# Second attention of a two-block transformer kernel: one query copy, each head's matmuls on its own 32 partitions

## Chip, cores and metric

The kernel runs on one core of a Trainium2 chip. The metric is the device time of one execution in microseconds (us). Before the change it is 2706.89 us, the median of 3 runs (2706.29 to 2707.69).

## What is computed

The input is a sequence of 2048 tokens of 128 features. Two pre-normed blocks follow each other: `x = x + attn1(layernorm(x))`, then `x = x + block2(layernorm(x))`.

The first attention has 16 heads of 64 features, with sinusoidal positions added to the keys. The second block is an attention with 16 heads of 8 features, an output projection, a layernorm, a router that gives each token one of four experts (relu MLPs with 512 hidden features) and a second layernorm. What matters here is its attention:

```python
q = (src @ Wq + bq).reshape(B, T, N_HEAD, HEAD_DIM)   # 2048 tokens, 16 heads of 8
k = (src @ Wk + bk).reshape(B, T, N_HEAD, HEAD_DIM)
v = (src @ Wv + bv).reshape(B, T, N_HEAD, HEAD_DIM)
scale = HEAD_DIM ** (-0.5)
scores = jnp.einsum('bqhd,bkhd->bhqk', q, k) * scale
probs = jax.nn.softmax(scores, axis=-1)
attn = jnp.einsum('bhqk,bkhd->bqhd', probs, v).reshape(B, T, D_MODEL)
```

All is float32. In the second block the query side's features are 8 per head; the kernel splits each float into a high part and a rest to keep precision in single-pass (fp32r) matmuls, so that a head takes 24 rows plus one row for the maximum, of 32.

## The kernel before

The kernel is written by hand engine by engine; its order is the order of the code, and semaphores tie the engines together. It has a startup and a loop for the first attention (to about 1590 us), a startup (1592 to 1674 us) and a loop (1674 to 2540 us) for the second, and a tail with the experts.

**Layout of the second attention.** The 16 heads make four groups of four. A group's keys lie in `k4` (line 167), 128 partitions by 2048 tokens: head h of the group has partitions 32h to 32h+31, of which 8 hold the high part, 8 the rest, 8 the high part again, and row 24 (`MROW`) a one. Queries come in 4 chunks of 512 tokens. They lie in `q4` (line 168), which takes up all of `kb`: for every chunk four copies of 128 partitions by 512, one per head, where only that head's 32 partitions are filled and the others are zero. So a matmul with all 128 rows of `k4` and one head's copy gives that head's scores. GpSimd zeroes `q4` once (line 758). VectorE computes a chunk's queries into `stage_q` by three operations (`parts2` and line 1120), and SP copies the four heads' 32 rows each by DMA (`move_q2`, lines 855 to 859). The row 24 of each copy gets minus the maximum of each query's scores (`move_m2`, line 861), so the exponential needs no further subtraction.

**Maxima.** Before a chunk's scores can be used, the maximum of each query's scores over all keys must be known. For the next chunk 64 tiles are computed (`max_tile2`, line 351): 4 heads x 4 query tiles of 128 x 4 key chunks of 512. Each is one matmul of 512 columns into a bank of `ring` (three PSUM banks, `RING = 3`), which VectorE reduces over its columns (line 993) and so releases. A tile may be written only when the tile three uses ahead of it has been released: `side()` (line 302) waits on `side_free` for that, for every use of the ring: tiles, query, key and value projections (lines 328, 342), the transposes of the output (line 527) and the finish of the maxima (line 360). TensorE and VectorE walk through the same list, `side_items2` (line 99), in the order of `TILES2` (line 96): all of head 0's tiles, then head 1's, and so on.

**The loop.** 16 chunks (4 groups x 4 query chunks), 16 steps each, one step per 128 keys. In step t TensorE runs the code of lines 565 to 587:

- `scores2` of step t+1 for heads 0 and 1 (two matmuls with 128 keys as weights and 512 queries as columns, line 511), once ScalarE has read these banks' former content;
- a part of the step's side items; `scores2` for heads 2 and 3; two more parts;
- `values2` of step t (line 518): four heads x two passes, 128 keys by 16 value columns, accumulated in `acc_o`, once ScalarE's exponentials of step t (line 676, two per step, 1024 columns each) are done;
- the last part of the side items.

The side items, 4 tiles in a plain step, are shared out evenly: `parts = share(on_pe(items), 4)`, so one of four tiles stands between the scores, one behind them and one ahead of the values, and one behind the values. Step 1 has the output transposes in addition, step 3 a query projection ("Q"), steps 6 and 10 key projections ("K") in the first two chunks of a group, step 6 the value projection ("V") in the third, step 12 the reduction over the key chunks ("mred") and the finish ("fin"), which transposes the maxima. From step 12 on the tiles are those of the chunk after the next ("early").

The startup computes the first chunk's queries, all the keys and values of the first group, then the first chunk's 64 tiles and 16 early ones.

Of the kernel before, what the change touches and what calls it, by code (L numbers as in the profile page):

```python
# [18 lines left out]
F32 = mybir.dt.float32  # L19
# [9 lines left out]
CW = 512  # L29
NC = S // CW  # L30
# [62 lines left out]

MAX2_STEPS = 12
EARLY2 = 4 * (STEPS2 - MAX2_STEPS)
TILES2 = [(h, q, k) for h in range(4) for q in range(QT) for k in range(NC)]


def side_items2(c, first):
# [49 lines left out]
def build(nc, x, w_pairs, wout_pairs, bqk_pairs, bv_pairs, b_out, pos, w_groups, bqk_groups, bv_groups,  # L149
          coefs, w_o, b_o, router_w, router_b, w1, b1, w2, b2, ln1_g, ln1_b, ln2_g, ln2_b, identity, out):  # L150
    ctx = ExitStack()
    with ctx:
# [12 lines left out]


        k4 = ka[:, :, 0, :]
        q4 = kb[:].rearrange("p a h n -> p (a h n)").rearrange("p (c h n) -> p c h n", c=NC, h=4)
        v1 = sb("v1", [128, 2, NT, 128])
        v1_flat = v1[:].rearrange("p a t n -> p (a t n)")  # L170
        v2_flat = v1_flat[:, 0:2 * NT * 4 * VW]
# [75 lines left out]
        exp2_done = [sem(f"exp2_done{h}") for h in range(2)]  # L247
        pv2_done, o2_copied, rs2_ready = sem("pv2_done"), sem("o2_copied"), sem("rs2_ready")
        mx2_ready, m2_dma = sem("mx2_ready"), sem("m2_dma")
        q2_part, q2_ready, q2_dma = sem("q2_part"), sem("q2_ready"), sem("q2_dma")  # L250
        k2_part, k2_ready = sem("k2_part"), sem("k2_ready")

        ld3, w2_ld, hid_ready = sem("ld3"), sem("w2_ld"), sem("hid_ready")
# [45 lines left out]
        def _(pe):  # L299
# [50 lines left out]

            def max_tile2(par, c, h, q, k):
                bank = side()
                nc.tensor.matmul(bank[:], q4[:, c, h, q * 128:(q + 1) * 128], k4[:, par, k * CW:(k + 1) * CW],  # L353
                                 start=True, stop=True).then_inc(side_full, 1)

            def fin(ready, count, n):
# [132 lines left out]
            for it in on_pe(start_items2()):  # L489
                kind = it[0]  # L490
                if kind == "Q":
                    proj(0, 0, it[1] * CW)
                elif kind == "K":
                    proj(0, 1, it[1] * CW)
                elif kind == "V":
                    proj_v2(0)
                elif kind == "max":
                    if it[1:] == TILES2[0]:
                        pe.wait_ge(q2_dma, 64)
                        pe.wait_ge(k2_ready, NC)  # L500
                    max_tile2(0, 0, *it[1:])
                elif kind == "early":
                    pe.wait_ge(q2_dma, 128)
                    max_tile2(0, 1, *it[1:])
                else:
                    fin(mx2_ready, 1, 16)

            def scores2(G, par, c, u, t):
                pe.wait_ge(exp2_done[u], 1 + STEPS2 * G + t)
                for k in range(2):  # L510
                    last = nc.tensor.matmul(sc[u][:, k, :], k4[:, par, t * 128:(t + 1) * 128], q4[:, c, 2 * u + k, :],  # L511
                                            start=True, stop=True)
                last.then_inc(sc2_ready[u], 1)

# [34 lines left out]

            def early_ready(g, c, G):  # L550

                pe.wait_ge(q2_dma, 64 * (G + 3))
                if c == 2:
                    pe.wait_ge(k2_ready, NC * (g + 2))

# [3 lines left out]
            with pe.Fori(0, GROUPS // 2) as i:  # L559
                rebase(LOOP2 + BODY2 * i, LOOP2 % RING)  # L560
                for k in range(2 * NC):
                    par, c = k // NC, k % NC
                    g = 2 * i + par
                    G = NC * g + c
                    for t, items in enumerate(side_items2(c, k == 0)):
                        parts = share(on_pe(items), 4)
                        nxt = (G, par, c, t + 1) if t < STEPS2 - 1 else (G + 1, (k + 1) // NC % 2, (k + 1) % NC, 0)
                        if t == STEPS2 - 1:
                            pe.wait_ge(m2_dma, 64 * (G + 2))
                        scores2(nxt[0], nxt[1], nxt[2], 0, nxt[3])  # L570
                        if t == MAX2_STEPS:
                            early_ready(g, c, G)
                        for it in parts[0]:
                            item2(it, g, par, c, k, G)
                        scores2(nxt[0], nxt[1], nxt[2], 1, nxt[3])
                        for it in parts[1]:
                            item2(it, g, par, c, k, G)
                        if t == 0:
                            pe.wait_ge(o2_copied, 1 + G)
                        for it in parts[2]:  # L580
                            item2(it, g, par, c, k, G)
                        for u in range(2):
                            pe.wait_ge(exp2_done[u], 1 + STEPS2 * G + t + 1)
                        values2(par, t, 0)
                        values2(par, t, 1).then_inc(pv2_done, 1)
                        for it in parts[3]:
                            item2(it, g, par, c, k, G)
                o_rows(G, k)


# [120 lines left out]
        def _(pool):  # L711
# [43 lines left out]
            pool.wait_ge(m_dma, 32 * (NC * PAIRS + 1))  # L755
            pool.wait_ge(q_dma, 96 * (NC * PAIRS + 2))
            pool.wait_ge(k_dma, 96 * NC * (PAIRS + 1))
            nc.gpsimd.memset(kb[:].rearrange("p a h n -> p (a h n)").bitcast(F32), 0.0).then_inc(init2, 1)
            nc.gpsimd.memset(v2_flat, 0.0).then_inc(init2, 1)
            pool.wait_ge(init2, 2)  # L760
            nc.gpsimd.memset(v2_flat.rearrange("p (x n) -> p x n", n=VW)[:, :, D2:D2 + 1], 1.0).then_inc(init2, 1)


# [1 line left out]
        def _(sp):  # L765
# [86 lines left out]
                sp.dma_start(tail_rows[:, 6 + e, :], b2[e:e + 1, :].to_broadcast([128, DM])).then_inc(ld3, 16)  # L852
            sp.dma_start(rb_sb[:], router_b[None, :].to_broadcast([128, 1])).then_inc(ld3, 16)

            def move_q2(n, c):
                sp.wait_ge(q2_ready, n + 1)
                for h in range(4):
                    rows = slice(32 * h, 32 * h + 32)
                    sp.dma_start(q4[rows, c, h, :].bitcast(F32), stage_q[rows, 0, :].bitcast(F32)).then_inc(q2_dma, 16)

            def move_m2(c, served):
                sp.wait_ge(side_free, served)
                for h in range(4):
                    sp.dma_start(q4[32 * h + MROW:32 * h + MROW + 1, c, h, :].bitcast(F32), m_rows[QT * h:QT * (h + 1), :].bitcast(F32)).then_inc(m2_dma, 16)

            sp.wait_ge(init2, 3)
            move_q2(0, 0)
            move_q2(1, 1)
            move_m2(0, START2 + NC + on_pe(start_items2()).index(("fin",)) + 1)
            with sp.Fori(0, GROUPS // 2) as i:  # L870
                for k in range(2 * NC):
                    par, c = k // NC, k % NC
                    g = 2 * i + par
                    G = NC * g + c
                    move_q2(G + 2, (c + 2) % NC)
                    if c == 2:
                        load_group(g + 2, par)
                    move_m2((c + 1) % NC, served2(i, k, "fin"))
# [1 line left out]
            sp.wait_ge(side_free, START3)  # L880

            sp.wait_ge(m2_dma, 64 * (NC * GROUPS + 1))
            sp.wait_ge(q2_dma, 64 * (NC * GROUPS + 2))
            sp.wait_ge(w2_dma, 48 * (GROUPS + 2))
            for e in range(E):
                sp.dma_start(w2_sb[:, e], w2[e].rearrange("(f k) n -> k f n", k=128)).then_inc(w2_ld, 16)
# [9 lines left out]
        def _(dve):  # L896
# [213 lines left out]
                dve.wait_ge(part, part_count)  # L1110
                done_so_far()

            def q2_proj(n, par):
                if not (isinstance(n, int) and n == 0):
                    dve.wait_ge(q2_ready, n)
                bank = side()
                parts2(bank, bqk_sb[:, par, 0:1], 0, stage_q[:, 1, :], accs[:, 0, :], q2_part, n + 1)
                if not (isinstance(n, int) and n == 0):
                    dve.wait_ge(q2_dma, 64 * n)
                nc.vector.scalar_tensor_tensor(stage_q[:, 0, :], stage_q[:, 1, :].bitcast(F32), coef_sb[:, 1:2],  # L1120
                                               accs[:, 0, :], ALU.mult, ALU.add).then_inc(q2_ready, 1)

            def k2_proj(n, par, c):
# [13 lines left out]
            for it in start_items2():  # L1137
                kind = it[0]
                if kind == "Q":
                    q2_proj(it[1], 0)  # L1140
                elif kind == "K":
                    k2_proj(it[1], 0, it[1])
                elif kind == "V":
                    dve.wait_ge(init2, 3)
                    v2_proj(0)
                elif kind == "mred":
                    mred(4, mx2_ready, mxp2[0])
                elif kind == "fin":
                    fin(0, 4, m2_dma)
                else:  # L1150
                    max_tile(*it[1:], mxp2[kind == "early"])
# [12 lines left out]
            with dve.Fori(0, GROUPS // 2) as i:  # L1164
                rebase(LOOP2 + BODY2 * i, LOOP2 % RING)
                for k in range(2 * NC):
# [3 lines left out]
                    for items in side_items2(c, k == 0):  # L1170
                        for it in items:
# [7 lines left out]
                            elif kind == "fin":  # L1179
                                fin(G + 1, 4, m2_dma)  # L1180
                            elif kind == "Q":
                                q2_proj(G + 2, par if c < 2 else 1 - par)
                            elif kind == "K":
                                if it[1] == 0:
                                    dve.wait_ge(w2_dma, 48 * (g + 2))
                                k2_proj(NC * (g + 1) + it[1], 1 - par, it[1])
                            elif kind == "V":
                                v2_proj(1 - par)
                            else:
                                o_rows(G - 1, g if c else g - 1, (c - 1) % NC)  # L1190
# [153 lines left out]
```

## Time and profile before

| | |
|---|---|
| median of 3 runs | 2706.89 us |
| span of the profiled execution | 2706.8 us |
| TensorE busy (PE) | 2573.3 us, 95% |
| weight loads (PEld) | 1447.8 us, 53% |
| VectorE busy (DVE) | 2049.9 us, 76% |
| ScalarE busy (ACT) | 1106.3 us, 41% |
| GpSimd busy (POOL) | 851.5 us, 31%, none of it after 1602 us |
| mean granted TensorE clock | 0.966 |
| DMA, mean share of the 16 engines | 11.1% |

The profile is of one execution, 2706.8 us from the first to the last instruction, 0.1 us from the median. Busy time of an engine is the time in which at least one of its instructions runs; matmuls are pipelined, so TensorE can be busy throughout and still have room, and the duration of one matmul (about 0.4 us for 512 columns) is longer than the distance to the next. L353 means line 353 of the kernel. The idle time of a group is that of its engine just ahead of it, with the engine and line that ended it. The granted clock is in parts of 2.4 GHz; 0.50 is 1.2 GHz.

### The profile page before, as it was taken

The numbers are of one execution on the slowest core, as the hardware profiler recorded it, in microseconds if no ns is written. First come the engines' busy times: TensorE is split into PE (matmuls) and PEld (weight loads), VectorE is DVE, ScalarE is ACT, GpSimd is POOL, SyncE is SP. The second block draws the span as 40 slices with busy tenths as digits, with TensorE's granted clock in tenths as the row PEclk, the third lists the DMA queues.
The fourth block names the chain that finished last, engine by engine and source line by source line (L and its number), as shares of the span: only waits on it lengthen the run. The fifth ranks groups of instructions, "written<-read, shape, count | busy, mean of one in ns | idle before, by whom it ended". The sixth has DMA issues, their size and how long they took to land. (4 is left out here: it accounts for less than half of the span.)

```text
span 2706.8 us, 39054 instructions
## 1 busy us (share of the span) xinstructions
PE 2573.3 (95%) x11918; PEld 1447.8 (53%) x11918; DVE 2049.9 (76%) x3471; ACT 1106.3 (41%) x1150; POOL 851.5 (31%) x405
## 2 busy tenths in 40 slices
PE   4999999999999999999999969999999999999796
PEld 2555555555555565555555544455455445455465
DVE  6767777676767767677776779988888888898834
ACT  0333333333333333343333311556556555665332
POOL 3463645646554645636465520000000000000000
PEclk8999999999999999999999976999999999999898
DMA  4120211211211201102112110000000000000000
GB/s 113 36 52 12 48 41 25 47 29 28 55 29 34 54 13 42 46 13 48 41 24 54 34 36 5 9 7 5 7 10 5 6 5 11 5 5 8 20 0 16
DMA packets 54408, 73.00 MB, mean 27 GB/s; under 512 B 12968, under 2 KB 23872, under 8 KB 54080
## 3 DMA queue, kind: packets, MB, share of 16 engines
q1 hardware_dynamic: 54208, 70.46, 11.1%
q8 instruction: 109, 1.79, 0.3%
q14 instruction: 91, 0.75, 0.1%
HBM read 9.33 MB, written 1.05 MB: 4 GB/s over the span
## 5 line engine op out<-in xcount | busy, mean ns | idle before, releaser
L993 DVE TENSOR_REDUCE mxp<-ring 128x1 f32<-128x512 f32 x1640 | 1068.3, 685 | 341.3 <-PE ring L348 292.4
L655 ACT ACTIVATE prob<-scores 128x1024 f32<-128x1024 f32 x512 | 524.0, 1025 | 902.1 <-PE scores L393 877.4
L676 ACT ACTIVATE prob<-scores 128x1024 f32<-128x1024 f32 x512 | 496.8, 1022 | 414.5 <-PE scores L511 414.3
L740 POOL TENSOR_TENSOR accp<-accp,prob 128x1024 f32<-128x1024 f32 x256 | 598.1, 2370 | 0.0
L400 PE MATMUL acc_o<-prob,v 128*64 128x512 f32 x2048 | 506.3, 616 | 0.0
L353 PE MATMUL ring<-ka,kb 128*128 128x512 f32 x1104 | 448.7, 450 | 9.9 <-DVE accs L1109 3.6
L392 PE MATMUL scores<-qa,ka 128*128 128x512 f32 x1028 | 425.7, 414 | 4.6 <-issue 3.1
L348 PE MATMUL ring<-ka,qa 128*128 128x512 f32 x1064 | 417.1, 436 | 11.9 <-DMA kb<-stage_k 7.9
L393 PE MATMUL scores<-qb,kb 65*128 65x512 f32 x1028 | 407.4, 396 | 0.0
L993 DVE TENSOR_REDUCE accs<-ring 128x1 f32<-128x512 f32 x528 | 343.5, 686 | 50.6 <-PE ring L353 49.7
L353 PEld LDWEIGHTS ring<-ka,kb 128*128 128x128 f32 x1104 | 213.7, 195 | 312.9 <-DVE mxp L993 132.7
L511 PE MATMUL scores<-kb,ka 128*128 128x512 f32 x1028 | 338.6, 411 | 4.5 <-ACT prob L676 4.5
L348 PEld LDWEIGHTS ring<-ka,qa 128*128 128x128 f32 x1064 | 192.2, 193 | 252.4 <-issue 106.5
L737 POOL TENSOR_TENSOR accp<-prob 128x1024 f32<-128x1024 f32 x64 | 151.3, 2364 | 549.9 <-DVE accs L1071 549.9
L518 PE MATMUL acc_o<-prob,v 128*16 128x512 f32 x2048 | 271.1, 601 | 0.0
L400 PEld LDWEIGHTS acc_o<-prob,v 128*64 128x64 f32 x2048 | 125.7, 137 | 237.8 <-issue 201.3
L392 PEld LDWEIGHTS scores<-qa,ka 128*128 128x128 f32 x1028 | 195.7, 190 | 57.2 <-issue 15.9
L511 PEld LDWEIGHTS scores<-kb,ka 128*128 128x128 f32 x1028 | 193.1, 190 | 53.1 <-issue 15.4
L393 PEld LDWEIGHTS scores<-qb,kb 65*128 65x128 f32 x1028 | 194.9, 190 | 48.0 <-issue 7.7
L1031 DVE TENSOR_TENSOR accp<-accp,prob 128x1024 f32<-128x1024 f32 x130 | 161.7, 1245 | 0.0
L1081 DVE SCALAR_TENSOR_TENSOR x<-ring,rs,x 128x128 f32<-128x128 f32 x264 | 74.3, 344 | 75.3 <-PE ring L421 75.3
L328 PE MATMUL ring<-xnt,w_sb 128*128 128x512 f32 x216 | 118.3, 635 | 4.6 <-issue 0.9
(105 smaller groups left out, 1366.1 us busy)
## 6 DMA issues: line engine op xcount, KB each, us to landing
ka<-stage_k SPq DMA_DIRECT2D x144, 128.0 KB, 2.3
qa<-stage_q SPq DMA_DIRECT2D x136, 128.0 KB, 2.3
kb<-stage_k SPq DMA_DIRECT2D x72, 128.0 KB, 2.3
qb<-stage_q SPq DMA_DIRECT2D x68, 128.0 KB, 2.3
kb<-stage_q SPq DMA_DIRECT2D x72, 64.0 KB, 2.0
w_sb<-w_pairs SPq DMA_DIRECT2D x10, 192.0 KB, 2.4
kb<-m_rows SPq DMA_DIRECT2D x68, 2.0 KB
qb<-m_rows SPq DMA_DIRECT2D x66, 2.0 KB
```

The costliest lines, as they stand in the source:

```text
L348: nc.tensor.matmul(bank[:], qa[:, c, h, q * 128:(q + 1) * 128], ka[:, par, h, k * CW:(k + 1) * CW], start=True, stop=True).then_inc(side_f ...
L353: nc.tensor.matmul(bank[:], q4[:, c, h, q * 128:(q + 1) * 128], k4[:, par, k * CW:(k + 1) * CW], start=True, stop=True).then_inc(side_full, 1)
L392: nc.tensor.matmul(sc[h][:, k, :], ka[:, par, h, keys_of], qa[:, c, h, :], start=True, stop=False)
L393: last = nc.tensor.matmul(sc[h][:, k, :], kb[0:D1 + 1, par, h, keys_of], qb[0:D1 + 1, c, h, :], start=False, stop=True)
L400: last = nc.tensor.matmul(acc_o[64 * h:64 * h + 64, :], v1[:, par, t, 64 * h:64 * h + 64], prob[:, h, j % 4, k, :], start=(t == 0), stop=( ...
L511: last = nc.tensor.matmul(sc[u][:, k, :], k4[:, par, t * 128:(t + 1) * 128], q4[:, c, 2 * u + k, :], start=True, stop=True)
L518: last = nc.tensor.matmul(acc_o[32 * h:32 * h + VW, :], v2[:, par, t, h, :], prob[:, u, t % 4, k, :], start=(t == 0), stop=(t == NT - 1))
L655: nc.scalar.activation(prob[:, h, j % 4, :, :], sc[h][:, :, :], ACT.Exp, scale=SCALE1).then_inc(exp_done[h], 1)
L676: nc.scalar.activation(prob[:, u, t % 4, :, :], sc[u][:, :, :], ACT.Exp, scale=SCALE2).then_inc(exp2_done[u], 1)
L740: nc.gpsimd.tensor_tensor(accp[:, h], accp[:, h], prob[:, h, j % 4], ALU.add).then_inc(pool_acc[h], 1)
L993: nc.vector.reduce_max(partial[:, h * QT + q, k:k + 1], bank[:], AX.X).then_inc(side_free, 1)
L1031: nc.vector.tensor_tensor(accp[:, h], accp[:, h], prob[:, h, j % 4], ALU.add).then_inc(done[h], 1)
```

## The change

The queries are kept once, not four times. Head h's score and maximum matmuls read only partitions 32h to 32h+31 of both operands (a contraction over 32 rows, not 128). The tiles' order becomes: for each query tile and key chunk, heads 2, 3, 0, 1. The side items of a step are shared into two parts, not four: after the scores of heads 0 and 1 come the first half (in a plain step the tiles of heads 2 and 3), after those of heads 2 and 3 the second (heads 0 and 1), and then the values. VectorE writes a chunk's queries straight to `q2`. The 72 copying DMAs, their semaphore `q2_dma` and the zeroing of `kb` go; the DMA of the maximum rows, one per head, stays.

```diff
-TILES2 = [(h, q, k) for h in range(4) for q in range(QT) for k in range(NC)]
+TILES2 = [(h, q, k) for q in range(QT) for k in range(NC) for h in (2, 3, 0, 1)]
...
-        q4 = kb[:].rearrange("p a h n -> p (a h n)").rearrange("p (c h n) -> p c h n", c=NC, h=4)
+        q2 = kb[:, 0, 0, :].rearrange("p (c n) -> p c n", c=NC)
...
             def max_tile2(par, c, h, q, k):
                 bank = side()
-                nc.tensor.matmul(bank[:], q4[:, c, h, q * 128:(q + 1) * 128], k4[:, par, k * CW:(k + 1) * CW],
+                rows = slice(32 * h, 32 * h + 32)
+                nc.tensor.matmul(bank[:], q2[rows, c, q * 128:(q + 1) * 128], k4[rows, par, k * CW:(k + 1) * CW],
                                  start=True, stop=True).then_inc(side_full, 1)
...
                 pe.wait_ge(exp2_done[u], 1 + STEPS2 * G + t)
                 for k in range(2):
-                    last = nc.tensor.matmul(sc[u][:, k, :], k4[:, par, t * 128:(t + 1) * 128], q4[:, c, 2 * u + k, :],
+                    rows = slice(32 * (2 * u + k), 32 * (2 * u + k) + 32)
+                    last = nc.tensor.matmul(sc[u][:, k, :], k4[rows, par, t * 128:(t + 1) * 128], q2[rows, c, :],
                                             start=True, stop=True)
                 last.then_inc(sc2_ready[u], 1)
...
-                        parts = share(on_pe(items), 4)
+                        parts = share(on_pe(items), 2)
...
                         if t == 0:
                             pe.wait_ge(o2_copied, 1 + G)
-                        for it in parts[2]:
-                            item2(it, g, par, c, k, G)
                         for u in range(2):
                             pe.wait_ge(exp2_done[u], 1 + STEPS2 * G + t + 1)
                         values2(par, t, 0)
                         values2(par, t, 1).then_inc(pv2_done, 1)
-                        for it in parts[3]:
-                            item2(it, g, par, c, k, G)
...
-            nc.gpsimd.memset(kb[:].rearrange("p a h n -> p (a h n)").bitcast(F32), 0.0).then_inc(init2, 1)
             nc.gpsimd.memset(v2_flat, 0.0).then_inc(init2, 1)
...
-            def move_q2(n, c):
-                sp.wait_ge(q2_ready, n + 1)
-                for h in range(4):
-                    rows = slice(32 * h, 32 * h + 32)
-                    sp.dma_start(q4[rows, c, h, :].bitcast(F32), stage_q[rows, 0, :].bitcast(F32)).then_inc(q2_dma, 16)
-
             def move_m2(c, served):
                 sp.wait_ge(side_free, served)
                 for h in range(4):
-                    sp.dma_start(q4[32 * h + MROW:32 * h + MROW + 1, c, h, :].bitcast(F32), m_rows[QT * h:QT * (h + 1), :].bitcast(F32)).then_inc(m2_dma, 16)
+                    sp.dma_start(q2[32 * h + MROW:32 * h + MROW + 1, c, :].bitcast(F32), m_rows[QT * h:QT * (h + 1), :].bitcast(F32)).then_inc(m2_dma, 16)
...
-                nc.vector.scalar_tensor_tensor(stage_q[:, 0, :], stage_q[:, 1, :].bitcast(F32), coef_sb[:, 1:2],
+                nc.vector.scalar_tensor_tensor(q2[:, c, :], stage_q[:, 1, :].bitcast(F32), coef_sb[:, 1:2],
                                                accs[:, 0, :], ALU.mult, ALU.add).then_inc(q2_ready, 1)
```

What waited for `q2_dma` (the first tiles of a chunk on TensorE, the next query chunk on VectorE, SP at the end) now waits for `q2_ready` or for nothing.

## Rows read from the trace of the kernel before

**Rows 1.** The windows view: busy us of PE, PEld, DVE, ACT, POOL; clock, DMA, GB/s.
```profile
1630.00:1660.00 30.00, 30.00 (x52) 14.46 (x51) 30.00 (x51) 0.00 (x0) 0.00 (x0) 0.50 0.02 5
1674.00:2540.00 866.00, 850.83 (x4375) 436.19 (x4375) 752.27 (x1192) 508.98 (x530) 0.00 (x0) 0.99 0.03 7
```

**Rows 2.** The groups by line, in the second attention's loop (1676 to 2540 us).
```profile
L353 PE MATMUL ring<-ka,kb 128*128 128x512 f32 x1024 | 401.9, 426 | 7.1 <-DVE accs L1109 3.0 <-DVE stage_kf L1109 3.0
L511 PE MATMUL scores<-kb,ka 128*128 128x512 f32 x1024 | 337.5, 411 | 4.5 <-ACT prob L676 4.5
L993 DVE TENSOR_REDUCE accs<-ring 128x1 f32<-128x512 f32 x513 | 334.4, 686 | 50.5 <-PE ring L353 49.5 <-issue 0.3
L993 DVE TENSOR_REDUCE mxp<-ring 128x1 f32<-128x512 f32 x512 | 333.6, 686 | 37.7 <-PE ring L353 37.4
L518 PE MATMUL acc_o<-prob,v 128*16 128x512 f32 x2048 | 271.1, 601 | 0.0
```

**Rows 3.** The waits in the same loop: us in total, times, longest.
```profile
ACT prob L676 <- PE scores L511: 414.3, 257, 72.2
```

**Rows 4.** The timeline of a plain step: start us, us, engine, line, operation [idle before].
```profile
1785.80 0.13 PEld L518 LDWEIGHTS acc_o<-prob,v 128*16 128x16 f32 x8 [0.35 <-ACT prob L676]
...
1786.78 0.50 PE L353 MATMUL ring<-ka,kb 128*128 128x512 f32 x1
...
1787.32 2.67 DVE L993 TENSOR_REDUCE accs<-ring 128x1 f32<-128x512 f32 x4 [0.35 <-PE ring L353]
...
1788.05 0.42 PEld L353 LDWEIGHTS ring<-ka,kb 128*128 128x128 f32 x2
1788.28 0.61 PE L353 MATMUL ring<-ka,kb 128*128 128x512 f32 x2
1788.82 0.13 PEld L518 LDWEIGHTS acc_o<-prob,v 128*16 128x16 f32 x8 [0.35 <-ACT prob L676]
```

**Rows 5.** The timeline of VectorE in the second attention's startup.
```profile
1627.47 38.35 DVE L993 TENSOR_REDUCE mxp<-ring 128x1 f32<-128x512 f32 x64
```

**Rows 6.** The DMA view's issues (KB, us to landing); GpSimd's timeline ahead of the startup.
```profile
kb<-stage_q SPq DMA_DIRECT2D x72, 64.0 KB, 2.0
...
1592.94 6.93 POOL L758 MEMSET kb<- 128x8192 f32 x1 [25.60 <-DVE x L1081]
```

**Rows 7.** Windows of line 421, first attention's end: PE (x), PEld (x), clock, DMA, GB/s.
```profile
1588.36:1589.38 1.02, 0.96 (x4) 0.96 (x5) 0.50 0.00 0
1589.38:1590.83 1.45, 1.45 (x12) 1.45 (x11) 0.50 0.00 0
```

**Rows 8.** The timeline of two steps around a query projection.
```profile
2122.53 0.13 PEld L518 LDWEIGHTS acc_o<-prob,v 128*16 128x16 f32 x8 [0.35 <-ACT prob L676]
...
2124.91 0.75 DVE L1108 TENSOR_SCALAR stage_q<-ring,bqk_sb 128x512 fp32r<-128x512 f32 x1 [0.17 <-PE ring L328]
...
2125.58 0.80 DVE L1109 TENSOR_SCALAR accs<-ring,bqk_sb,coef_sb 128x512 f32<-128x512 f32 x1
...
2126.43 0.19 PEld L353 LDWEIGHTS ring<-ka,kb 128*128 128x128 f32 x1 [0.61 <-DVE accs L1109]
...
2126.86 0.13 PEld L518 LDWEIGHTS acc_o<-prob,v 128*16 128x16 f32 x8 [0.25 <-issue]
...
2127.24 4.27 DVE L993 TENSOR_REDUCE accs<-ring 128x1 f32<-128x512 f32 x7
...
2130.21 0.13 PEld L518 LDWEIGHTS acc_o<-prob,v 128*16 128x16 f32 x8 [0.25 <-ACT prob L676]
```

**Rows 9.** The timeline of weight loads: values behind a step with transposes; around a finish.
```profile
1792.29 0.13 PEld L518 LDWEIGHTS acc_o<-prob,v 128*16 128x16 f32 x8 [0.36 <-ACT prob L676]
...
2090.85 0.13 PEld L518 LDWEIGHTS acc_o<-prob,v 128*16 128x16 f32 x8 [0.35 <-ACT prob L676]
...
2097.05 0.13 PEld L518 LDWEIGHTS acc_o<-prob,v 128*16 128x16 f32 x8 [0.24 <-ACT prob L676]
```

**Rows 10.** Line 353 in the startup at the lower clock (min/median/max ns).
```profile
L353 PE MATMUL ring<-ka,kb x18: 792/794/796, 1639.6 to 1649.7; 128*128 128x512 f32 x18
```

More of the change, by code:

```diff
@@ L249, in build @@
         mx2_ready, m2_dma = sem("mx2_ready"), sem("m2_dma")
-        q2_part, q2_ready, q2_dma = sem("q2_part"), sem("q2_ready"), sem("q2_dma")
+        q2_part, q2_ready = sem("q2_part"), sem("q2_ready")
         k2_part, k2_ready = sem("k2_part"), sem("k2_ready")
@@ L498, in _ @@
                     if it[1:] == TILES2[0]:
-                        pe.wait_ge(q2_dma, 64)
+                        pe.wait_ge(q2_ready, 1)
                         pe.wait_ge(k2_ready, NC)
@@ L502, in _ @@
                 elif kind == "early":
-                    pe.wait_ge(q2_dma, 128)
+                    pe.wait_ge(q2_ready, 2)
                     max_tile2(0, 1, *it[1:])
@@ L550, in early_ready @@
             def early_ready(g, c, G):
-                pe.wait_ge(q2_dma, 64 * (G + 3))
+                pe.wait_ge(q2_ready, G + 3)
                 if c == 2:
@@ L757, in _ @@
             pool.wait_ge(k_dma, 96 * NC * (PAIRS + 1))
-            nc.gpsimd.memset(kb[:].rearrange("p a h n -> p (a h n)").bitcast(F32), 0.0).then_inc(init2, 1)
             nc.gpsimd.memset(v2_flat, 0.0).then_inc(init2, 1)
-            pool.wait_ge(init2, 2)
+            pool.wait_ge(init2, 1)
             nc.gpsimd.memset(v2_flat.rearrange("p (x n) -> p x n", n=VW)[:, :, D2:D2 + 1], 1.0).then_inc(init2, 1)
@@ L863, in move_m2 @@
                 for h in range(4):
-                    sp.dma_start(q4[32 * h + MROW:32 * h + MROW + 1, c, h, :].bitcast(F32), m_rows[QT * h:QT * (h + 1), :].bitcast(F32)).then_inc(m2_dma, 16)
-            sp.wait_ge(init2, 3)
-            move_q2(0, 0)
-            move_q2(1, 1)
+                    sp.dma_start(q2[32 * h + MROW:32 * h + MROW + 1, c, :].bitcast(F32), m_rows[QT * h:QT * (h + 1), :].bitcast(F32)).then_inc(m2_dma, 16)
             move_m2(0, START2 + NC + on_pe(start_items2()).index(("fin",)) + 1)
@@ L874, in _ @@
                     G = NC * g + c
-                    move_q2(G + 2, (c + 2) % NC)
                     if c == 2:
@@ L882, in _ @@
             sp.wait_ge(m2_dma, 64 * (NC * GROUPS + 1))
-            sp.wait_ge(q2_dma, 64 * (NC * GROUPS + 2))
             sp.wait_ge(w2_dma, 48 * (GROUPS + 2))
@@ L1111, in parts2, with q2_proj @@
                 done_so_far()
-            def q2_proj(n, par):
+            def q2_proj(n, par, c):
                 if not (isinstance(n, int) and n == 0):
@@ L1117, in q2_proj @@
                 parts2(bank, bqk_sb[:, par, 0:1], 0, stage_q[:, 1, :], accs[:, 0, :], q2_part, n + 1)
-                if not (isinstance(n, int) and n == 0):
-                    dve.wait_ge(q2_dma, 64 * n)
-                nc.vector.scalar_tensor_tensor(stage_q[:, 0, :], stage_q[:, 1, :].bitcast(F32), coef_sb[:, 1:2],
+                nc.vector.scalar_tensor_tensor(q2[:, c, :], stage_q[:, 1, :].bitcast(F32), coef_sb[:, 1:2],
                                                accs[:, 0, :], ALU.mult, ALU.add).then_inc(q2_ready, 1)
@@ L1139, in _ @@
                 if kind == "Q":
-                    q2_proj(it[1], 0)
+                    q2_proj(it[1], 0, it[1])
                 elif kind == "K":
@@ L1143, in _ @@
                 elif kind == "V":
-                    dve.wait_ge(init2, 3)
+                    dve.wait_ge(init2, 2)
                     v2_proj(0)
@@ L1181, in _ @@
                             elif kind == "Q":
-                                q2_proj(G + 2, par if c < 2 else 1 - par)
+                                q2_proj(G + 2, par if c < 2 else 1 - par, (c + 2) % NC)
                             elif kind == "K":
```

## The prediction

> **What bounds the kernel now.** I read the busy time by stretch first. Only the second attention is touched, so its loop has to be explained: 866 us of the 2706.8 us span, TensorE busy 850.8, VectorE 752.3, ScalarE 509.0, at a granted clock of 0.99 [rows 1]. In the groups by line TensorE's time there is 1024 maximum tiles (402 us), 1024 score matmuls (338 us) and 2048 value matmuls (271 us) [rows 2]. The waits agree: exponentials wait for scores, 414 us (72 of it once, ahead of the loop) [rows 3], and reductions for a tile, 49.5 + 37.4 us [rows 2]. ScalarE, busy 59% of the loop, can't be the bound.
>
> A plain step in the timeline shows how it runs. From one values block to the next is 3.02 us (1785.80 to 1788.82). The eight 512-column matmuls ahead of the values follow each other 0.23 us apart (the last two tiles: weight load 1788.05, matmul 1788.28). From the values to the next weight load it takes 0.98 us (1785.80 to 1786.78). VectorE's four reductions take 2.67 us of it, and it idles 0.35 us ahead of the first [rows 4]. TensorE is the bound, VectorE close behind: back to back it does 64 reductions in 38.35 us, 0.60 us each, 2.40 us a step [rows 5].
>
> **The change, part by part.**
>
> *Copies, DMAs, memset gone.* 72 DMAs from SP (2.0 us to landing each) and one memset of 6.93 us [rows 6]. A chunk's copies are made after step 3 and first read in step 12. The memset ends at 1599.87 [rows 6]; the value tile that waits for it stands just ahead of the 64 startup tiles, which begin at 1627.47 [rows 5]. I cost all of it at 0: without that cover it would be 7 us, once. VectorE's three operations for a query chunk stay, with another destination; the maximum row's four DMAs stay; nothing is moved past another on a queue.
>
> *Row groups.* Head h now reads partitions 32h to 32h+31 alone. Does the array run such matmuls side by side? For column groups the value matmuls show it: 601 ns each, yet 2048 in 271 us, 132 ns apiece [rows 2]. For row groups there is one place: the end of the first attention, where the output matmuls of the two 64-row halves come one behind the other. While the first half's run alone, four take 1.02 us; with the second half's beside them, twelve take 1.45 us, 0.12 us apiece at the same clock of 0.50, with eleven weight loads [rows 7]. Matmuls and weight loads of different row groups overlap. So four in a row (score, score, tile, tile, on four different groups) are one pass of 0.23 us here, loads side by side. The other end is no overlap at all, 0.23 us each. Between them: matmuls overlap, loads go one by one, at 0.11 us if four in 1.02 us at half clock [rows 7] are the pace of loads. I take the first end, the nearest row.
>
> The Trainium skill (TensorE: Matmul & The Clock Gate, Part 3) has measured 3.07 times, not 4, for four 32-row matmuls of 512 columns. By it a pass takes some 0.07 us more and the sum below loses about 18 us. No run here has groups of 32 rows.
>
> *The order of a step* decides how much of that arrives. Before, one of the four tiles went behind the values; now all four go ahead: S0 S0 m1 m2, S1 S1 m3 m4, values. The ring has three banks, so m4 waits until VectorE has released m1 of the same step, and the values are queued behind m4. The chain, from a step's first weight load:
> - m1's load 0.05 (estimate: two loads close together ahead of it), its matmul 0.50, hand-over to VectorE 0.04 (1786.78 + 0.50 to 1787.32) [rows 4]: its reduction starts at 0.59.
> - The reduction 0.69 [rows 2], release to the waiting load 0.05 (VectorE's operation ends at 2126.38, the tile that waited for it loads at 2126.43) [rows 8]: m4 loads at 1.33.
> - From a load that had to wait to the values 0.43 (2126.43 to 2126.86) [rows 8], values to the next load 0.98 [rows 4].
>
> Sum 2.74 us, 0.28 less than 3.02, though TensorE's own work falls by more than 1 us. ScalarE's two exponentials (509 us over 256 steps, 2.0) [rows 1] and VectorE's 2.40 fit in.
>
> *Steps with more in them.* A query or key projection waits for m2's release (0.59 + 0.60 + 0.69 + 0.05 = 1.93); VectorE starts on it at about 3.1 and takes 2.33 (2124.91 to 2127.24) [rows 8]. The next m1 is reduced only at 5.4, its m4 loads at 6.1, and the step after begins 1.41 later, at 7.5. Before, such a pair took 7.68 (2122.53 to 2130.21) [rows 8]: gain 0.15. A step with output transposes: o waits for the same 1.93, four transposes 0.6, values 0.98: 3.5, before 3.47 (1788.82 to 1792.29) [rows 4, 9]: 0. The finish of the maxima: before 6.20 for two steps (2090.85 to 2097.05) [rows 9]; after, fin stands behind the reduction of all maxima and e4 behind e2, which I put at 6.1 to 6.3: 0. The value projection is one long TensorE piece before and after: 0.
>
> *Sum.* 256 steps: 32 projection pairs (64), 15 with transposes, 16 with a finish (8 of them with a plain neighbour), 4 value projections, about 1 at the loop's turn: 148 plain. 148 x 0.28 = 41.4, 32 x 0.15 = 4.8: 46 us. Startup tiles run at VectorE's 0.60 us either way [rows 5]. 2706.8 - 46 = 2661. The span lies 0.1 us from the median of the runs (2706.89), so nothing is corrected.
>
> **Rivals.**
>
> *Loads one by one.* m1's load comes at 0.22 and the chain is 2.93: 148 x 0.09 = 13 won, some 0.05 to 0.25 lost in each special step, 11 in all: about 2704, no change. Against it: the eleven loads in 1.45 us [rows 7]. Chance 0.07.
>
> *No overlap (slower).* m1 stands behind two scores, so its reduction starts at 1.0, not 0.59, m4 loads at 1.74, the step takes 3.15. The tile that used to hide behind the values is then pure loss: 148 x 0.13 = 19, pairs 7.95 (9), transposes (7), finishes and value projections (10): 2752. It decides from where m1's reduction starts later than about 0.80 after the first load. For it: what rows 7 show is groups of 64 rows, not of 32. That the matmuls don't land on separate groups at all is the same case. Chance 0.09.
>
> *The clock falls (slower).* With one tile per 0.6 us in the startup the granted clock stood at 0.50, the 1.2 GHz level; in the dense loop it is at 0.99, near all of it at 2.4 GHz [rows 1]. The new step leaves TensorE without a matmul for about 0.6 us while m4 waits, and each matmul uses a quarter of the rows. At half clock a tile takes 0.79 [rows 10] and the values block would double, the step comes to about 4.3, 1.55 more: 30 of 256 steps there eat the whole gain. With a quarter of them, 2661 + 99 = 2760. Against it: the startup had 512 columns in 0.6 us, the new loop has well over twice that. The Trainium skill (TensorE: Matmul & The Clock Gate, Part 1) says that activity releases the throttle and that it is back when the engine idles: this rival; the trace agrees with its two levels. Chance 0.10.
>
> *m4's wait is hidden.* Were the chain shorter than VectorE's work, a plain step would be 2.40: 148 x 0.62, about 2610. No row shortens it. Chance 0.04.
>
> **The numbers.** The forecast keeps 0.70: 2661 us, its own range 2640 to 2695 (0.1 us on the chain moves 15 to 25 us). To leave out no more than 2 in 10 the range runs from 2635 to 2715, past the one-by-one loads and short of the two slow cases. A measurement here can tell 0.2%, 5.4 us, from no change. Faster 0.70 + 0.04 = 0.74, same 0.07, slower 0.19.
>
> **What the profile after would show.** Right: 2.7 to 2.8 us from values block to values block in plain steps; the weight loads of two scores and two tiles within 0.1 us; TensorE without a matmul ahead of the fourth tile, released by the first tile's reduction; values straight behind it; VectorE busy some 92% of the loop, idle only ahead of m1; the loop's clock still about 0.99; projection pairs near 7.5. Wrong: loads 0.11 or 0.23 us apart; stretches at 0.50 inside the loop beyond those it has; a plain step at 2.4 or over 3.0.

## The result, and the profile after

The changed kernel takes 2776.12 us (median of 4 runs, 2748.06 to 2820.05); beside it the kernel before took 2707.29 us (2706.29 to 2707.80). The ratio is 1.022, with a 95% interval of 1.017 to 1.027: 2.2% slower. Here and below a median is that of all runs, while a ratio leaves out runs over 1.5% above the fastest of their kernel (here the one at 2820.05 us). The forecast was 2661 us, faster. The profiled execution has a span of 2766.9 us. That the runs lie 72 us apart, and those of before 1.5 us, already belongs to the cause: the time goes with the mean granted clock, 2748.06 us at 0.912, 2768.73 at 0.902, 2783.52 at 0.894, 2820.05 at 0.878.

The head and the second part of the page of the changed kernel (40 equal slices; PEclk is the granted clock in tenths):

```profile
span 2766.9 us, 38971 instructions
PE 2520.2 (91%) x11918; PEld 1266.8 (46%) x11918; DVE 2017.9 (73%) x3471; ACT 1104.5 (40%) x1150; POOL 844.9 (31%) x404
...
PE   5999999999999999999999978898888888888696
...
PEclk8899999999999999999999956758977797597898
```

The first attention (slices 2 to 23) runs as before. In the second the clock row has fives and sevens, and TensorE is no longer busy all the time. The windows view of the changed kernel, for its loop and two stretches in it:

```profile
1674.00:2600.00 926.00, 794.54 (x4360) 251.70 (x4357) 720.61 (x1186) 502.78 (x526) 0.00 (x0) 0.80 0.01 2
1810.00:1880.00 70.00, 64.68 (x271) 22.21 (x267) 39.11 (x66) 29.66 (x31) 0.00 (x0) 0.50 0.00 1
1900.00:2000.00 100.00, 82.01 (x532) 27.43 (x532) 91.70 (x152) 62.89 (x67) 0.00 (x0) 1.00 0.01 1
```

The loop's clock is 0.80, against 0.99 in [rows 1]. VectorE does 66 operations in the 70 us at 0.50 (1.06 us each) and 152 in the 100 us at 1.00 (0.66 us each). The groups by line, which answer to [rows 2]:

```profile
L354 PE MATMUL ring<-ka,kb 32*128 32x512 f32 x1015 | 398.8, 573 | 122.2 <-DVE mxp L979 61.0 <-DVE accs L979 59.5
L520 PE MATMUL acc_o<-prob,v 128*16 128x512 f32 x2032 | 336.5, 741 | 0.0
L979 DVE TENSOR_REDUCE mxp<-ring 128x1 f32<-128x512 f32 x512 | 318.4, 682 | 82.2 <-PE ring L354 81.9
L979 DVE TENSOR_REDUCE accs<-ring 128x1 f32<-128x512 f32 x502 | 312.2, 682 | 88.7 <-PE ring L354 88.6
L513 PE MATMUL scores<-kb,ka 32*128 32x512 f32 x1016 | 227.7, 528 | 3.6 <-ACT prob L674 3.6
```

TensorE now idles 122 us ahead of tiles, nearly all of it waiting for VectorE, where it was 7.1 us before, and VectorE waits twice as long for tiles as before (171 us for 88): each waits for the other in turn. The value matmuls, whose code is unchanged, take 741 ns each and not 601: that is the clock.

The timeline of one plain step at full clock, which answers to [rows 4]:

```profile
1906.83 0.13 PEld L520 LDWEIGHTS acc_o<-prob,v 128*16 128x16 f32 x8 [0.25 <-issue]
...
1907.81 0.18 PEld L513 LDWEIGHTS scores<-kb,ka 32*128 32x128 f32 x2 [0.85 <-issue]
...
1907.82 0.29 PEld L354 LDWEIGHTS ring<-ka,kb 32*128 32x128 f32 x3
...
1908.39 2.48 DVE L979 TENSOR_REDUCE accs<-ring 128x1 f32<-128x512 f32 x4 [0.66 <-PE ring L354]
1909.13 0.18 PEld L354 LDWEIGHTS ring<-ka,kb 32*128 32x128 f32 x1 [1.02 <-DVE accs L979]
...
1909.56 0.13 PEld L520 LDWEIGHTS acc_o<-prob,v 128*16 128x16 f32 x8 [0.24 <-ACT prob L674]
```

(PEld is a weight load, `x3` three of them joined in one line.) Weights of scores and tiles load 0.01 us apart, the first reduction starts 0.58 us after the first load, the fourth tile loads 1.32 us after that same load, the values follow 0.43 later: 2.73 us from values to values, as forecast (2.74). And a plain step at half clock:

```profile
1831.31 0.15 PEld L520 LDWEIGHTS acc_o<-prob,v 128*16 128x16 f32 x8 [0.44 <-ACT prob L674]
...
1833.15 0.28 PEld L513 LDWEIGHTS scores<-kb,ka 32*128 32x128 f32 x2 [1.69 <-issue]
...
1834.02 2.48 DVE L979 TENSOR_REDUCE accs<-ring 128x1 f32<-128x512 f32 x4 [1.69 <-PE ring L354]
1834.76 0.28 PEld L354 LDWEIGHTS ring<-ka,kb 32*128 32x128 f32 x1 [1.11 <-DVE accs L979]
...
1835.48 0.15 PEld L520 LDWEIGHTS acc_o<-prob,v 128*16 128x16 f32 x8 [0.44 <-ACT prob L674]
```

4.17 us, 1.44 more. About 74 of the loop's 256 steps are of this kind (steps over 0.6 us above the shortest of their place in a chunk). From the first to the last values block the loop takes 923.8 us (1675.0 to 2598.8), against 858.0 before (1678.5 to 2536.5). At full clock throughout it would take about 805 (each place in a chunk at its shortest time, four chunks summed and taken four times); the same sum for the kernel before gives about 847. So at full clock the change brings some 42 us, and half clock costs the loop 119 us where it cost 11.

The kernel before shows what is new in this. Its clock falls too, four times in the loop, three of them in a value projection and one at the loop's turn, and it is back after at most 7 us. One of its falls, by the windows view:

```profile
1810.50:1813.70 3.20, 3.20 (x11) 2.72 (x11) 1.38 (x2) 1.02 (x1) 0.00 (x0) 0.50 0.00 0
```

In the changed kernel it falls eleven times in the loop, five of them in the plain step behind a query projection, two behind a key projection, three in a value projection and one at the turn, and stays down for up to 72 us; eight of the eleven stretches end in or just behind a projection. At half clock are 371 us of the loop, before 17.

### The profile page after: what moved, and what is told of

Same layout as the page of the kernel before. It is cut to its first block, busy times and chain, and to the rows that moved or that the text cites. A ratio compares the mean times of both kernels' runs of the same rounds, so it can differ in the third digit from the quotient of the medians.

```text
span 2766.9 us, 38971 instructions
## 1 busy us (share of the span) xinstructions
PE 2520.2 (91%) x11918; PEld 1266.8 (46%) x11918; DVE 2017.9 (73%) x3471; ACT 1104.5 (40%) x1150; POOL 844.9 (31%) x404
## 4 chain that ended last, share of the span: by engine, by line
PE 68%; DVE 22%; issue 8%; SPq 1%; DVEq 1%; DMA 1%; POOL 0%; ACT 0%; ACTq 0%; POOLq 0%
PE acc_o L401 14%; DVE mxp L979 11%; PE acc_o L520 11%; PE ring L348 7%; PE ring L354 6%; PE scores L393 6%; PE scores L394 5%; PE scores L513 5%; DVE accs L979 3%; PE ring L328 3%; PE ring L422 3%; PE acc_o L622 2%; PE ring L411 2%; PE scores L613 2%; DVE accp L1017 2%
## 5 line engine op out<-in xcount | busy, mean ns | idle before, releaser
L979 DVE TENSOR_REDUCE mxp<-ring 128x1 f32<-128x512 f32 x1640 | 1053.1, 683 | 384.4 <-PE ring L348 290.8
L354 PE MATMUL ring<-ka,kb 32*128 32x512 f32 x1104 | 450.8, 589 | 125.0 <-DVE mxp L979 61.7
L979 DVE TENSOR_REDUCE accs<-ring 128x1 f32<-128x512 f32 x528 | 328.0, 682 | 90.7 <-PE ring L354 90.6
L520 PE MATMUL acc_o<-prob,v 128*16 128x512 f32 x2048 | 338.6, 740 | 0.0
L354 PEld LDWEIGHTS ring<-ka,kb 32*128 32x128 f32 x1104 | 180.4, 222 | 285.0 <-DVE mxp L979 138.9
L513 PE MATMUL scores<-kb,ka 32*128 32x512 f32 x1028 | 231.1, 530 | 4.7 <-ACT prob L674 4.7
L513 PEld LDWEIGHTS scores<-kb,ka 32*128 32x128 f32 x1028 | 94.7, 223 | 290.8 <-issue 284.2
L328 PE MATMUL ring<-xnt,w_sb 128*128 128x512 f32 x216 | 130.9, 694 | 7.9 <-DVE stage_kf L1095 1.1
```

Source lines behind the costliest of these rows:

```text
L354: nc.tensor.matmul(bank[:], q2[rows, c, q * 128:(q + 1) * 128], k4[rows, par, k * CW:(k + 1) * CW], start=True, stop=True).then_inc(side_f ...
L513: last = nc.tensor.matmul(sc[u][:, k, :], k4[rows, par, t * 128:(t + 1) * 128], q2[rows, c, :], start=True, stop=True)
L520: last = nc.tensor.matmul(acc_o[32 * h:32 * h + VW, :], v2[:, par, t, h, :], prob[:, u, t % 4, k, :], start=(t == 0), stop=(t == NT - 1))
L979: nc.vector.reduce_max(partial[:, h * QT + q, k:k + 1], bank[:], AX.X).then_inc(side_free, 1)
```

## The experiments

The profile after leaves two theories. **Gap**: the clock falls because TensorE has no matmul while m4 waits, and at half clock the loop isn't dense enough to win it back. **Rows**: a matmul over 32 rows does less to hold the clock than one over 128, however dense the stream.

### The new order with all 128 rows

On the kernel before:

```diff
-TILES2 = [(h, q, k) for h in range(4) for q in range(QT) for k in range(NC)]
+TILES2 = [(h, q, k) for q in range(QT) for k in range(NC) for h in (2, 3, 0, 1)]
...
-                        parts = share(on_pe(items), 4)
+                        parts = share(on_pe(items), 2)
```

(and the loops over the third and fourth part go).

> The kernel before (padded query copies, 128-row matmuls) with the new tile order and all four tiles ahead of the values. Gap theory (the clock falls because TensorE waits, without a matmul, for the fourth tile's bank, and at half clock the loop is not dense enough to win it back): here TensorE is busy all along, so the loop keeps a clock of 0.99 and the plain step is the 3.15 us that my chain gives without overlap, about 2752 us. Row theory (32-row matmuls do not hold the clock, however dense): the same, all rows are in use. If the order costs nothing: 3.02 us and 2707 us, and my chain is wrong.

2760.58 us, 1.0197 of before (1.018 to 1.022). Two values blocks and the loop's window:

```profile
1787.45 0.13 PEld L518 LDWEIGHTS acc_o<-prob,v 128*16 128x16 f32 x8 [0.24 <-issue]
...
1790.60 0.13 PEld L518 LDWEIGHTS acc_o<-prob,v 128*16 128x16 f32 x8 [0.24 <-issue]
```

```profile
1674.00:2430.00 756.00, 738.41 (x3596) 358.99 (x3600) 597.79 (x986) 422.64 (x438) 0.00 (x0) 0.99 0.03 6
```

The step is 3.15 us, the chain's own number without overlap (3.15), at a clock of 0.99. So the new order alone (of the tiles and of the step together) costs 53 us: by the chain it is the fourth tile, moved from behind the values to ahead of them, that is the loss, and the overlap has to earn it back first.

### All heads on the same 32 rows

On the changed kernel:

```diff
-                rows = slice(32 * h, 32 * h + 32)
+                rows = slice(0, 32)
...
-                    rows = slice(32 * (2 * u + k), 32 * (2 * u + k) + 32)
+                    rows = slice(0, 32)
```

> The changed kernel, but every head's score and maximum matmuls read rows 0 to 31 (the output is that of the first head's scores for all four), so no two of them can overlap: a dense stream of 32-row matmuls. Gap theory: clock about 0.99 in the loop, plain step 3.15 us, about 2750 us. Row theory: the clock falls for much of the loop, the time is over 2850 us.

3161.64 us (3094.33 to 3225.90), 17% over the 2708.01 us of before beside it; the fastest of its four runs is still 14% over. The loop's window, and two values blocks where the clock was up:

```profile
1674.00:2430.00 756.00, 748.38 (x2453) 351.74 (x2451) 418.43 (x671) 298.26 (x299) 0.00 (x0) 0.61 0.01 1
```

```profile
2154.17 0.13 PEld L520 LDWEIGHTS acc_o<-prob,v 128*16 128x16 f32 x8 [0.25 <-issue]
2157.33 0.13 PEld L520 LDWEIGHTS acc_o<-prob,v 128*16 128x16 f32 x8 [0.25 <-issue]
```

A stretch at full clock here, and one of the run above:

```profile
2138.00:2198.00 60.00, 58.87 (x285) 27.49 (x285) 50.17 (x83) 33.68 (x35) 0.00 (x0) 1.00 0.02 4
```

```profile
2150.00:2270.00 120.00, 117.20 (x563) 55.12 (x564) 99.74 (x163) 66.00 (x69) 0.00 (x0) 1.00 0.03 7
```

This settles it against the gap theory in its pure form. At full clock the step is 3.16 us, against 3.15 in the run above, with the same stream of matmuls, TensorE busy 98% of the time in both (58.87 of 60 us, 117.20 of 120); the difference is 32 rows or 128. One loop holds 0.99, the other has 0.61. Rows count, and they count even where they carry zeros: in the run above 96 of the 128 rows of a query copy are zero. Without overlap the step at half clock is long (5.5 us), so each stretch costs more. No run has full rows with a gap, so what a gap does by itself is not shown.

### Filling the wait

The two score matmuls of heads 2 and 3 are issued three times over (the result is the same):

```diff
-                for k in range(2):
+                for k in (0, 1) * (3 if u else 1):
                     rows = slice(32 * (2 * u + k), 32 * (2 * u + k) + 32)
```

> The changed kernel; the two score matmuls of heads 2 and 3 are issued three times over (same result), which fills TensorE's wait for the fourth tile and is off the chain of the step. Gap theory: plain step still 2.73 us, clock in the loop 0.98 or more, 2655 to 2675 us. Row theory: the added matmuls have 32 rows as well, the stretches at 0.50 stay, 2740 us or more.

2663.42 us (2660.16 to 2669.82), 0.984 of before (0.982 to 0.986). The loop's window and a plain step's start:

```profile
1674.00:2430.00 756.00, 697.01 (x4908) 282.36 (x4906) 657.55 (x1081) 459.12 (x479) 0.00 (x0) 0.96 0.01 2
```

```profile
1904.88 0.63 PE L513 MATMUL scores<-kb,ka 32*128 32x512 f32 x4
...
1905.63 0.18 PEld L354 LDWEIGHTS ring<-ka,kb 32*128 32x128 f32 x1 [0.55 <-DVE accs L979]
```

The added matmuls lie in the wait, the fourth tile still loads 1.32 us after the step's first load (1904.31), and the clock is 0.96 instead of 0.79 in the same window of the changed kernel. So the rows theory, as far as it said that only rows matter, falls too: 32-row matmuls help, if there are more of them. One reading fits the three runs, that rows and time without a matmul count together; it is a reading and not shown, and the run with one tile behind the values, below, does not follow from it.

The same kernel once more, on another chip:

> The scores three times over once more, on the chip and beside the runs of the short reductions: 2655 to 2675 us as the first time, so that the gain over the kernel before does not rest on one session.

2673.56 us (2664.31 to 2683.60), 0.988 of before (0.986 to 0.990). The gain stands, at 1.2% to 1.6%; the median lies inside the expectation, two runs of five above it, the farther by 9 us.

### One tile behind the values again

On the changed kernel, the four-part order of before:

```diff
-                        parts = share(on_pe(items), 2)
+                        parts = share(on_pe(items), 4)
...
+                        for it in parts[2]:
+                            item2(it, g, par, c, k, G)
...
                         values2(par, t, 1).then_inc(pv2_done, 1)
+                        for it in parts[3]:
+                            item2(it, g, par, c, k, G)
```

> The changed kernel with the side items shared into four parts as before, so that one tile stands behind the values. The chain from the tile behind the values over its reduction to the fourth tile ahead of the next values is as long, 2.69 us, so both theories expect no more than 0.05 us from it in a step at full clock, and the same falls of the clock: 2740 to 2820 us. If the place of the tile were what costs, this would come to 2665 us.

2890.77 us (2855.39 to 2949.99), 1.062 of before (1.055 to 1.069): outside what both theories expected. The step at full clock is 2.69 us as expected, but the clock in the loop's window is 0.66. In its query steps the projection stands behind the values, at half clock such a step takes 6.9 us and the clock stayed low through most of them, while in the changed kernel the projection and the values follow each other and the clock often rises there. That this is why is argued and not shown; no run separates it.

### Full-row fillers

In place of the repeated scores, one or two 128-row matmuls, each into a bank that the scores then overwrite (two in the cut below; `range(1 if u else 0)` for one):

```diff
+                for k in range(2 if u else 0):
+                    nc.tensor.matmul(sc[u][:, k, :], k4[:, par, t * 128:(t + 1) * 128], q2[:, c, :],
+                                     start=True, stop=True)
                 for k in range(2):
```

> The changed kernel with one 128-row matmul of 512 columns ahead of the two score matmuls of heads 2 and 3, in the bank that they then overwrite. It fills half as much of TensorE's wait as the four added 32-row matmuls of the run with scores three times, which take two passes. If time without a matmul is what lowers the clock, the clock in the loop lies between the changed kernel's 0.80 and that run's 0.96. If the clock goes by rows as well, one full matmul is worth four of 32 rows: the clock is 0.96 or more, 2655 to 2670 us.

> Two such 128-row matmuls in a step. Rows count: the stretches at 0.50 that were left behind the value projections go, clock 0.99, and if two passes and the changes between full-row and 32-row matmuls fit into the wait of 0.7 us, the plain step is 2.75 to 2.85 us, 2650 to 2680 us in all. Only time without a matmul counts: like the scores three times, clock 0.96.

One: 2681.81 us (2673.79 to 2683.58), 0.989 of before (0.988 to 0.991). Two: 2667.14 us (2660.65 to 2676.24), 0.985 (0.983 to 0.987). The windows of the two loops, in this order:

```profile
1674.00:2430.00 756.00, 723.14 (x4145) 241.44 (x4148) 656.78 (x1079) 457.30 (x477) 0.00 (x0) 0.95 0.01 2
```

```profile
1674.00:2430.00 756.00, 730.08 (x4454) 269.05 (x4453) 664.55 (x1089) 484.47 (x482) 0.00 (x0) 0.97 0.01 2
```

One pass over 128 rows does nearly what two passes over 2 x 32 rows do (0.95 and 0.96). But by what I had asked of these two runs neither proves rows. One filler is short of the 0.96 and slower than the 2655 to 2670 us that I named for rows; 0.95 also lies where the gap theory put it. With two the clock is 0.97, between the 0.99 of rows and the 0.96 of gaps, and short stretches at 0.50 are left. It is the pair of runs on full rows and on one row group that shows rows.

In these kernels the clock falls only where it also fell before, at a value projection or the loop's turn, and the stretches differ in length: up to 20.5 us with the scores three times (17 us in the second profile), 10 to 17 us with one full-row matmul, at most 7 us with two, as in the kernel before. The stretch behind a value projection in the kernel with two fillers:

```profile
1810.10 0.15 PEld L523 LDWEIGHTS acc_o<-prob,v 128*16 128x16 f32 x8
1814.54 0.15 PEld L523 LDWEIGHTS acc_o<-prob,v 128*16 128x16 f32 x8 [0.44 <-issue]
1818.18 0.13 PEld L523 LDWEIGHTS acc_o<-prob,v 128*16 128x16 f32 x8 [0.24 <-ACT prob L677]
1820.90 0.13 PEld L523 LDWEIGHTS acc_o<-prob,v 128*16 128x16 f32 x8 [0.25 <-ACT prob L677]
```

4.44, 3.64, and then 2.72 us again. The plain step is 2.73, just under the 2.75 to 2.85 expected.

### The value projection made dense

On the changed kernel:

```diff
                 elif kind == "V":
-                    proj_v2(1 - par)
+                    proj(1 - par, 1, 0)
```

> The changed kernel; in the loop the value projection's 32 short matmuls are left out and one dense two-pass matmul stands in their place (the values of the later groups are therefore not those of the reference). If the sparse value projection is what starts most long stretches at half clock, the chunks behind it run at 2.73 us a step: 2680 to 2715 us, clock in the loop 0.90 or more, 12 us of which are the projection's own time. If the clock falls anywhere in a plain step, 2740 us or more.

2693.22 us (2645.80 to 2717.00); its fastest run is 102 us below the fastest of the changed kernel. The runs go with the mean granted clock again: 0.961 in the fastest, 0.923 in the slowest, which is the profiled one. There the clock in the window is 0.85, against 0.79 in the changed kernel and the 0.90 or more that I had asked for. Part of it is right: the steps behind the value projection run at 2.73 us. Part of the gain is the projection's own time, 3.96 us for its step in place of 6.79 to 11.14. And the clock still falls eight times in the loop, five of them in the plain step behind a query projection; the two longest stretches, 58 and 72 us, begin away from the value projection. So the sparse value projection is one trigger and not the only one.

### A shorter reduction

On the kernel with two fillers, for the tiles of the second attention (the loop's calls change in the same way as the startup's, shown here):

```diff
+            def max_tile_short(h, q, k, partial):
+                bank = side()
+                nc.vector.reduce_max(partial[:, h * QT + q, k:k + 1], bank[:, 0:384], AX.X).then_inc(side_free, 1)
...
-                    max_tile(*it[1:], mxp2[kind == "early"])
+                    max_tile_short(*it[1:], mxp2[kind == "early"])
```

> The kernel with two full-row fillers; in the second attention VectorE reduces 384 of a tile's 512 columns, so a quarter of the keys is left out of the maxima. If the plain step is the chain over the first tile's reduction, it shortens by the 128 columns that the reduction no longer reads (0.13 us by the 0.69 us of 512 columns less a fixed part): 2.58 to 2.62 us, 2630 to 2650 us in all. If ScalarE, TensorE's own work or the fillers set the step, it stays 2.73 us and 2667 us.

2611.26 us (2608.43 to 2614.24), 0.964 of before (0.962 to 0.965). A plain step:

```profile
1905.12 0.13 PEld L523 LDWEIGHTS acc_o<-prob,v 128*16 128x16 f32 x8 [0.24 <-ACT prob L677]
...
1906.68 2.12 DVE L986 TENSOR_REDUCE mxp<-ring 128x1 f32<-128x384 f32 x4 [0.48 <-PE ring L354]
...
1907.72 0.13 PEld L523 LDWEIGHTS acc_o<-prob,v 128*16 128x16 f32 x8 [0.25 <-issue]
```

The reduction takes 0.55 us instead of 0.68, and the step 2.60 instead of 2.73: one for one. VectorE does four reductions in a step, so if its own work were the bound the step would have lost 0.52 us: the chain over the first tile's reduction is the bound. The total fell further than the 2630 to 2650 us expected, since the steps around projections shortened too (3.96 us to 3.69, the first of a pair) and the second attention's first values block comes 16 us earlier (1666.2 for 1682.6), since the startup's tiles are reduced over 384 columns as well. It is a measurement and not a version to use as it is: with other data a left-out score could be far above the maximum that is subtracted.

## Why the prediction was wrong

- **The sign was wrong, and the step that failed is the clock**: the rival "the clock falls", chance 0.10, which I priced at 2760 us with a quarter of the steps at half clock. The forecast of 2661 keeps the loop's clock at about 0.99, a loss of nothing; it was 0.80, and half clock cost 119 us. The rival came out at 2776 with about 74 of 256, 1.44 us each and not 1.55. What misled me is the sentence against it, that the startup had 512 columns in 0.6 us and the new loop well over twice that: I weighed all columns alike, though a matmul over 32 rows does less to hold the clock. The runs on one row group (0.61) and on full rows (0.99) show that. Nor had I seen that half clock can last: 7 us at most before, up to 72 us after. Why it lasts is open. The step is then 4.17 us long with the same work in it, and in the plain steps nothing denser comes, but no run isolates this.
- **Overlap of row groups**: right. Loads 0.01 us apart, in place of the 0.05 in all that I took. (In the rival of loads one by one the load's price is misread: four matmuls in 1.02 us at half clock give 0.13 us at full clock and not 0.11, and 0.22 us for the loads would give 2.91 and not 2.93. The forecast does not use it.)
- **The chain of a step**: right, 2.73 for 2.74; without overlap 3.15 for 3.15; shorter by just what the reduction loses (0.13 us). m4's wait for m1's release is its middle.
- **VectorE's share**: right where the clock is up, 91.7 of 100 us (1900 to 2000 us) for the 92% forecast; over the whole loop it is 720.6 of 926 us.
- **Steps with more in them**: a projection pair 3.96 + 3.51 = 7.47 us at full clock for 7.5, transposes 3.49 for 3.5, the finish and the step behind it 3.33 + 2.73 = 6.06 for 6.1 to 6.3. The value projection, put at no change, is where a stretch at half clock begins in three groups of four.
- **Copies, DMAs, memset at 0**: no run isolates them; nothing in the profile after contradicts it. The DMAs' absence shows in the loop's DMA share, 0.01 for 0.03.
- **The sum**: right but for the clock. At full clock the loop would take about 805 us for 847 before, 42 us, where I had 46. With two fillers, which nearly hold the clock, the loop takes 815.0 us (1682.6 to 2497.6) and the kernel 2667, near the 2661 forecast.
- The Trainium skill's 3.07 (TensorE: Matmul & The Clock Gate, Part 3) would by my estimate from it have put 0.07 us more on a step. The trace doesn't show it: the tile's reduction starts 0.58 us after the first load, 0.04 later than behind a single tile before (0.54, [rows 4]), and the step takes 2.73 us. Its sentence in Part 1 that activity releases the throttle was the one to take more seriously. The traces agree that the clock follows what the array does, and show that being busy is not enough: 0.61 against 0.99 for the same stream on 32 and on 128 rows, TensorE busy 98% at full clock in both.

## What to carry to other kernels

Packing matmuls into row groups makes TensorE finish sooner only if something else then lets it go on: write down the chain through the ring of banks (first tile, its reduction, the tile that waits for that bank, what is queued behind it) before counting matmul time. And ask what is left of the array's work when a dense loop on 128 rows becomes a loose one on 32: where the granted clock can fall, a few matmuls without use, put into a wait off the chain, gained 94 to 113 us here over the same loop without them and made it 1.1% to 1.6% faster than before. Look at the spread of runs as well: 72 us between runs of the changed kernel, where those of before lie 1.5 to 9 us apart, says that something beside the order of instructions has a part in the time, and the granted clock of each run names it.

## What the hardware showed that I had not expected

- The clock depends on rows: the same dense stream, TensorE busy 98% and 3.15 us a step at full clock, holds 0.99 on 128 rows (96 of them zero in the queries) and has 0.61 on 32.
- Half clock can last: six stretches of 31 to 72 us in the changed kernel's loop, and five shorter ones, which begin at or just behind a projection but for one at the loop's turn. With two 128-row fillers a step, as in the kernel before, none in the loop is over 7 us.
- Four weight loads for four row groups start within 0.01 us, 0.18 us each, as the fourth tile's alone.
- Open: why one tile behind the values lowers the clock to 0.66 when its step at full clock is no longer (2.69 us).
